# Reordering the opening of a graph layer: transfers, projections and the first matmuls

## The chip, the cores and the metric

The kernel runs on one core of one Trainium2 chip. The metric is the device time in microseconds (us) of one execution. TensorE does the matmuls, VectorE, ScalarE and GpSimd (POOL in the rows) the element-wise work, SyncE (SP) issues the transfers, and 16 DMA engines carry them out.

## The reference

```python
h = item_feat @ W_item.T + b_item            # 10000 x 128
b = x @ W_user.T + b_user                    # 10000 x 128
y = relu(adj @ h + b)                        # adj: 10000 x 10000, float32
m = mean(x + y); v = var(x + y)              # per row
out = (x + y - m) / sqrt(v + 1e-5)
```

Nearly all the work, and nearly all the bytes (400 MB), is `adj @ h`.

## The kernel before, in words

The 10000 users are cut into 20 groups of 500, the 10000 items into 79 chunks of 128 rows (the last has 16). One more chunk holds the user's own projection: `x` stands as its "adj" and `w_user` as its "h". The 80 chunks make 20 tiles of four. One `adj` tile of a group is 128 x 4 x 500 floats, 1.024 MB.

float32 products are made from two float32r halves. ScalarE rounds a tile (`adj_hi`, L301), VectorE subtracts what was rounded (`adj_lo`, L403), and TensorE adds three products for each chunk: hi x hi (L242), lo x hi (L243), and, once `adj_lo` is there, hi x lo (L246). That is `tile_product`. The `h` side is split likewise: ScalarE makes `h_hi` (L342), GpSimd `h_lo` (L367).

`h` is made during group 0. `project_items(t)` (L227) multiplies the four chunks of item tile t by `w_item` into a PSUM bank `h_ps`; VectorE adds the bias into `h_full` (L383), and then the two casts follow. Before, item tile t+2 is projected ahead of the product of tile t, so product 0 has projections 0, 1 and 2 in front of it. The PSUM ring has two banks, `items` two slots, `h_full` three.

What sets the order is each engine's own instruction list, written by hand, with semaphores between the lists. A list is executed in order, so an instruction that waits holds all behind it. SP issues all transfers on one queue. `load_items(t)` waits until the projection that last used its slot is done; `load_adj(g, t)` waits until the `adj_lo` of five tiles earlier is made. One semaphore, `weights_landed`, counts the four small transfers `w_item`, `bias_item`, `w_user` and `bias_user`, and TensorE, ScalarE and VectorE all wait for 64, which is all four.

The results of a group are finished during the next one: relu, adding `x`, transposes by TensorE into `z_ps` with the identity `ident` (L256), statistics, normalisation and the store. Only group 19 does this after the last product. GpSimd makes `ident` at the very start.

## Time and profile before

| | |
|---|---|
| time, median of 3 runs | 1142.09 us (1141.98 to 1143.6) |
| span of the profiled execution, first to last instruction | 1140.9 us |
| the profiled execution's own time | not given apart from its span |
| TensorE busy | 1121.9 us (98%) |
| VectorE, ScalarE, GpSimd busy | 942.8, 805.8, 34.0 us |
| DMA | 415.91 MB, 365 GB/s over the span |
| mean granted TensorE clock | 0.995 |

TensorE's busy time counts from a matmul's start to its modelled end, so a share of 98% says that it hardly ever had nothing queued, not that the array is at its peak. The granted clock is in parts of 2.4 GHz; 0.50 is 1.2 GHz. The "idle before" of a row names what released the engine.

### The profile page before, as it was taken

The page shows a single profiled execution, that of the slowest core. Times are in us where ns is not written, and L with a number is a line of the kernel's source. Part 1 is how long each engine was busy: PE and PEld are TensorE (multiplying, and loading weights), DVE is VectorE, ACT ScalarE, POOL GpSimd, SP SyncE. Part 2 cuts the span into 40 slices and gives each one's busy share as a digit, 9 for nine tenths or more (in the row PEclk, how much of TensorE's full clock was granted, in tenths as well). Part 3 has the DMA queues.
Part 4 walks back from the last instruction along what each step waited for, and adds up shares of the span by engine and source line. Part 5 has one row for each costly group of instructions (what it writes and reads, how often), then busy time and mean ns, then how long its engine had stood idle before and what let it go on. Part 6 is the DMA issues. An engine that isn't in the chain of part 4 may idle for free. (4 is left out here: it accounts for less than half of the span.)

```text
span 1140.9 us, 14807 instructions
## 1 busy us (share of the span) xinstructions
PE 1121.9 (98%) x5038; PEld 931.9 (82%) x5038; DVE 942.8 (83%) x684; ACT 805.8 (71%) x583; POOL 34.0 (3%) x27
## 2 busy tenths in 40 slices
PE   6999999999999999999999999999999999999997
PEld 5888888888888888888888888888888888888885
DVE  4889888888888888888888887888888888888884
ACT  5677767677767777776777777767777777676764
POOL 3440000000000000000000000000000000000000
PEclk8999999999999999999999999999999999999999
DMA  8999999999999999999999999999999999999992
GB/s 297 352 367 402 391 378 368 375 375 378 371 367 382 373 369 379 369 372 374 367 382 365 370 365 392 359 392 362 379 362 387 369 374 368 387 364 366 383 374 78
DMA packets 67471, 415.91 MB, mean 365 GB/s; under 512 B 7872, under 2 KB 11264, under 8 KB 67456
## 3 DMA queue, kind: packets, MB, share of 16 engines
q1 hardware_dynamic: 67456, 415.71, 95.6%
q8 instruction: 9, 0.15, 0.0%
q14 instruction: 6, 0.05, 0.0%
HBM read 410.44 MB, written 5.24 MB: 364 GB/s over the span
## 5 line engine op out<-in xcount | busy, mean ns | idle before, releaser
L403 DVE TENSOR_TENSOR adj_lo<-adj,adj_hi 128x2000 fp32r<-128x2000 f32 (+1 forms) x400 | 873.0, 2191 | 131.1 <-ACT adj_hi L301 130.9
L301 ACT CAST adj_hi<-adj 128x2000 fp32r<-128x2000 f32 (+1 forms) x400 | 730.7, 1827 | 294.3 <-PE acc L246 262.0
L242 PE MATMUL acc<-adj_hi,h_hi 128*128 128x500 f32 x1600 | 630.0, 394 | 0.2 <-POOL h_lo L367 0.2
L243 PE MATMUL acc<-adj_hi,h_lo 128*128 128x500 f32 x1600 | 622.4, 389 | 0.0
L246 PE MATMUL acc<-adj_lo,h_hi 128*128 128x500 f32 x1600 | 429.1, 388 | 0.0
L242 PEld LDWEIGHTS acc<-adj_hi,h_hi 128*128 128x128 f32 x1600 | 301.4, 188 | 63.0 <-POOL h_lo L367 0.5
L246 PEld LDWEIGHTS acc<-adj_lo,h_hi 128*128 128x128 f32 x1600 | 301.1, 188 | 62.1
L243 PEld LDWEIGHTS acc<-adj_hi,h_lo 128*128 128x128 f32 x1600 | 301.9, 189 | 60.6
L418 DVE BATCH_NORM_STATS2 stats<-z_ps 128x6 f32<-128x128 f32 x80 | 17.8, 285 | 32.1 <-PE z_ps L256 32.1
L227 PE MATMUL h_ps<-w_item,items 128*128 128x128 f32 (+1 forms) x158 | 23.3, 296 | 11.1 <-DMA bias_user<-b_user 6.6
L367 POOL TENSOR_TENSOR h_lo<-h_full,h_hi 128x512 fp32r<-128x512 f32 (+1 forms) x20 | 32.8, 1643 | 43.3 <-ACT h_hi L342 43.3
L227 PEld LDWEIGHTS h_ps<-w_item,items 128*128 128x128 f32 (+1 forms) x158 | 22.5, 209 | 12.7 <-DMA bias_user<-b_user 6.6
L383 DVE TENSOR_TENSOR h_full<-h_ps,bias_item 128x512 f32<-128x512 f32 (+1 forms) x20 | 13.6, 678 | 21.6 <-PE h_ps L227 21.6
L320 ACT ACTIVATE normed<-z_ps,shift,rstd 128x128 f32<-128x128 f32 x80 | 29.9, 454 | 0.4 <-DVE shift L436 0.4
L296 ACT CAST adj_hi<-adj 128x500 fp32r<-128x500 f32 x20 | 12.2, 612 | 17.9 <-PE acc L246 17.9
L410 DVE TENSOR_TENSOR z_t<-relu_t,xg 128x500 f32<-128x500 f32 x20 | 13.5, 674 | 7.9 <-ACT relu_t L307 7.9
L307 ACT ACTIVATE relu_t<-acc,bias_user 128x500 f32<-128x500 f32 x20 | 13.4, 671 | 8.8 <-PE acc L246 8.8
L396 DVE TENSOR_TENSOR adj_lo<-adj,adj_hi 128x500 fp32r<-128x500 f32 x20 | 14.3, 715 | 0.0
L342 ACT CAST h_hi<-h_full 128x512 fp32r<-128x512 f32 (+1 forms) x20 | 12.2, 608 | 3.0 <-DVE h_full L383 3.0
L256 PE MATMUL z_ps<-ident,z_t 128*128 128x128 f32 x80 | 12.0, 273 | 1.5 <-DVE z_t L410 1.5
L398 DVE TENSOR_TENSOR adj_lo<-xg,adj_hi 128x500 fp32r<-128x500 f32 x20 | 13.5, 673 | 0.0
L256 PEld LDWEIGHTS z_ps<-ident,z_t 128*128 128x128 f32 x80 | 9.9, 141 | 4.2 <-DVE z_t L410 1.9
(19 smaller groups left out, 37.0 us busy)
## 6 DMA issues: line engine op xcount, KB each, us to landing
adj<-adj_t SPq DMA_DIRECT2D x380, 1000.0 KB, 7.3
adj<-adj_t SPq DMA_DIRECT2D x20, 500.0 KB, 5.5
out<-normed SPq DMA_DIRECT2D x20, 256.0 KB, 7.6
xg<-x_t SPq DMA_DIRECT2D x20, 250.0 KB, 4.4
items<-item_t SPq DMA_DIRECT2D x19, 256.0 KB, 4.7
adj<-adj_tail SPq DMA_DIRECT2D x20, 31.2 KB, 4.8
items<-item_t SPq DMA_DIRECT2D x1, 136.0 KB, 4.5
w_item<-w_item_t SPq DMA_DIRECT2D x1, 64.0 KB, 1.8
```

Source lines behind the costliest of these rows:

```text
L227: mm = nc.tensor.matmul(h_ps[t % 2][0:m, c, :], items[:, t % ITEM_RING, c * P:c * P + m], w_item[:, :], start=True, stop=True)
L242: nc.tensor.matmul(into, h_hi[:, k, :], adj_hi[:, s, c, :], start=(k == 0), stop=False)
L243: nc.tensor.matmul(into, h_lo[:, k, :], adj_hi[:, s, c, :], start=False, stop=False)
L246: mm = nc.tensor.matmul(into, h_hi[:, chunk(t, c), :], adj_lo[:, s, c, :], start=False, stop=(t == LAST and c == PER_TILE - 1))
L256: mm = nc.tensor.transpose(z_ps[:, b, :], z_t[:, b, :], ident[:, :])
L301: nc.scalar.copy(adj_hi[:, s, start:, :], adj[:, a, start:, :]).then_inc(hi_made, 1)
L320: ins = nc.scalar.activation(normed[:, b, :], z_ps[:, b, :], ACT.Identity, bias=shift[:, b:b + 1], scale=rstd[:, b:b + 1])
L367: nc.gpsimd.tensor_tensor(h_lo[:, k:k + n, :], h_full[:, t % H_RING, 0:n, :], h_hi[:, k:k + n, :].bitcast(F32), ALU.subtract).then_inc(h_l ...
L383: ins = nc.vector.tensor_tensor(h_full[:, s, 0:n, :], h_ps[t % 2][:, 0:n, :], bias_item[:, None, :].to_broadcast([P, n, HID]), ALU.add)
L396: nc.vector.tensor_tensor(adj_lo[:, s, AT_TAIL, :], adj[:, a, AT_TAIL, :], adj_hi[:, s, AT_TAIL, :].bitcast(F32), ALU.subtract)
L403: nc.vector.tensor_tensor(adj_lo[:, s, start:, :], adj[:, a, start:, :], adj_hi[:, s, start:, :].bitcast(F32), ALU.subtract).then_inc(lo_m ...
L418: ins = nc.vector.bn_stats(stats[:, b, :], z_ps[:, b, :])
```

## The change

The four small transfers are issued by ScalarE on its own queue, each with a semaphore of its own. SP begins with items 0, 1 and 2, then adj 0, items 3, 4 and 5, adj 1, and from there the items of tile t+4 ahead of adj t. TensorE makes nine transposes of `ident` into `z_ps` as soon as `ident` is ready, waits for `w_item` alone, and projects six item tiles before product 0; later projection t+5 stands ahead of product t. The rings grow: `items` 3, `h_full` 4, `h_ps` 4. VectorE adds the bias of four tiles ahead of the first `adj_lo`, ScalarE casts three `h_full` tiles ahead of the first `adj_hi`. The halves of `w_user` are made with the last tile.

```diff
@@ constants
-ITEM_RING = 2
-H_RING = 3
+ITEM_RING = 3
+H_RING = 4
+H_PS_RING = 4
+LEAD = 6
+WARM = 9
@@ tiles and semaphores
-        h_ps = [psum(f"h_ps{i}", [P, PER_TILE, HID]) for i in range(2)]
+        h_ps = [psum(f"h_ps{i}", [P, PER_TILE, HID]) for i in range(H_PS_RING)]
...
-        weights_landed = sem("weights_landed")
+        w_item_landed = sem("w_item_landed")
+        bias_item_landed = sem("bias_item_landed")
+        w_user_landed = sem("w_user_landed")
+        bias_user_landed = sem("bias_user_landed")
@@ SP
-            sp.dma_start(w_item[:, :], w_item_t).then_inc(weights_landed, 16)
             load_items(0)
-            sp.dma_start(bias_item[:, :], b_item.rearrange("(a n) -> a n", a=1).to_broadcast([P, HID])).then_inc(weights_landed, 16)
             load_items(1)
-            sp.dma_start(w_user[:, :], w_user_t).then_inc(weights_landed, 16)
-            sp.dma_start(bias_user[:, :], b_user.rearrange("(p a) -> p a", a=1)).then_inc(weights_landed, 16)
-            for t in range(TILES):
-                if t >= ITEM_RING:
-                    load_items(t)
+            load_items(2)
+            load_adj(0, 0)
+            load_items(3)
+            load_items(4)
+            load_items(5)
+            load_adj(0, 1)
+            for t in range(2, TILES):
+                if t + LEAD - 2 < TILES:
+                    load_items(t + LEAD - 2)
                 if t == LOAD_X_AT:
                     load_x(0)
                 load_adj(0, t)
@@ TensorE
-                if t >= 2:
-                    pe.wait_ge(h_full_made, t - 1)
+                if t >= H_PS_RING:
+                    pe.wait_ge(h_full_made, t - H_PS_RING + 1)
...
-            pe.wait_ge(weights_landed, 64)
-            project_items(0)
-            project_items(1)
+            def warm_up():
+
+                for b in range(WARM):
+                    nc.tensor.transpose(z_ps[:, b % BLOCKS, :], ident[:, :], ident[:, :])
+
+            pe.wait_ge(ident_ready, 1)
+            warm_up()
+            pe.wait_ge(w_item_landed, 16)
+            for t in range(LEAD):
+                project_items(t)
             for t in range(TILES):
-                if t + 2 < TILES:
-                    project_items(t + 2)
+                if 1 <= t and t + LEAD - 1 < TILES:
+                    project_items(t + LEAD - 1)
                 if t == LAST:
                     pe.wait_ge(w_lo_made, 1)
                 pe.wait_ge(h_lo_made, t + 1)
                 tile_product(0, t, 0)
-            pe.wait_ge(ident_ready, 1)
@@ ScalarE
-            act.wait_ge(weights_landed, 64)
-            nc.scalar.copy(h_hi[:, CHUNKS - 1, :], w_user[:, :]).then_inc(w_hi_made, 1)
+            def split_h(t):
+
+                n = item_chunks(t)
+                act.wait_ge(h_full_made, t + 1)
+                nc.scalar.copy(h_hi[:, t * PER_TILE:t * PER_TILE + n, :],
+                               h_full[:, t % H_RING, 0:n, :]).then_inc(h_hi_made, 1)
+
+            act.dma_start(w_item[:, :], w_item_t).then_inc(w_item_landed, 16)
+            act.dma_start(bias_item[:, :], b_item.rearrange("(a n) -> a n", a=1).to_broadcast([P, HID])).then_inc(bias_item_landed, 16)
+            act.dma_start(w_user[:, :], w_user_t).then_inc(w_user_landed, 16)
+            act.dma_start(bias_user[:, :], b_user.rearrange("(p a) -> p a", a=1)).then_inc(bias_user_landed, 16)
+            for t in range(LEAD - 3):
+                split_h(t)
             act.wait_ge(pads_ready, 1)
             for t in range(TILES):
+                if t == LAST:
+                    act.wait_ge(w_user_landed, 16)
+                    nc.scalar.copy(h_hi[:, CHUNKS - 1, :], w_user[:, :]).then_inc(w_hi_made, 1)
+                    act.wait_ge(bias_user_landed, 16)
                 split_hi(0, t)
...
+                if t + LEAD - 3 < TILES:
+                    split_h(t + LEAD - 3)
@@ GpSimd: the h_lo of w_user moves behind the loop over tiles
@@ VectorE
-            dve.wait_ge(weights_landed, 64)
-            add_item_bias(0)
-            add_item_bias(1)
+            dve.wait_ge(bias_item_landed, 16)
+            for t in range(LEAD - 2):
+                add_item_bias(t)
             for t in range(TILES):
                 split_lo(0, t)
-                if t + 2 < TILES:
-                    add_item_bias(t + 2)
+                if t + LEAD - 2 < TILES:
+                    add_item_bias(t + LEAD - 2)
```

The first rows of SP's list before; the names are destination and source of each transfer, and "waits" the semaphore:

```order
L198 DMA w_item<-w_item_t 128x128
L169 DMA items<-item_t 128x512
L200 DMA bias_item<-b_item 128x128
L169 DMA items<-item_t 128x512
L202 DMA w_user<-w_user_t 128x128
L203 DMA bias_user<-b_user 128x1
L178 DMA adj<-adj_t 128x2000 x2
L169 DMA items<-item_t 128x512 [waits h_product]
L178 DMA adj<-adj_t 128x2000
```

And SP's list now, to the same depth:

```order
L175 DMA items<-item_t 128x512 x3
L184 DMA adj<-adj_t 128x2000
L175 DMA items<-item_t 128x512 [waits h_product] x3
L184 DMA adj<-adj_t 128x2000
L175 DMA items<-item_t 128x512 [waits h_product]
L184 DMA adj<-adj_t 128x2000
```

The small transfers are gone from it, one adj tile instead of two stands ahead of the first items that wait for a projection (`h_product`), and three items stand between adj 0 and adj 1.

TensorE's list before, from its start to the lo part of product 0:

```order
L227 MATMUL h_ps<-w_item,items 128x128 [waits item_landed0,weights_landed]
L227 MATMUL h_ps<-w_item,items 128x128 x3
L227 MATMUL h_ps<-w_item,items 128x128 [waits item_landed1]
...
L227 MATMUL h_ps<-w_item,items 128x128 [waits h_full_made,item_landed0]
...
L242 MATMUL acc<-adj_hi,h_hi 128x500 [waits hi_made,h_lo_made]
...
L246 MATMUL acc<-adj_lo,h_hi 128x500 [waits lo_made]
```

The same stretch now:

```order
L278 MATMUL z_ps<-ident 128x128 [waits ident_ready]
L278 MATMUL z_ps<-ident 128x128 x8
L235 MATMUL h_ps<-w_item,items 128x128 [waits item_landed0,w_item_landed]
...
L235 MATMUL h_ps<-w_item,items 128x128 [waits item_landed1]
...
L235 MATMUL h_ps<-w_item,items 128x128 [waits item_landed2]
...
L235 MATMUL h_ps<-w_item,items 128x128 [waits item_landed0]
...
L235 MATMUL h_ps<-w_item,items 128x128 [waits h_full_made,item_landed1]
...
L235 MATMUL h_ps<-w_item,items 128x128 [waits h_full_made,item_landed2]
...
L250 MATMUL acc<-adj_hi,h_hi 128x500 [waits hi_made,h_lo_made]
...
L254 MATMUL acc<-adj_lo,h_hi 128x500 [waits lo_made]
```

Three projections moved ahead of product 0, the nine transposes ahead of everything, and the first projection now waits for `w_item` where it waited for all four small transfers.

## Rows read from the trace of the kernel before

**Rows 1.** The page, part 1: busy time, share of the span, instructions.
```profile
PE 1121.9 (98%) x5038; PEld 931.9 (82%) x5038; DVE 942.8 (83%) x684; ACT 805.8 (71%) x583; POOL 34.0 (3%) x27
```

**Rows 2.** Waits of the whole run: engine, line, releaser: us in total, times, longest.
```profile
ACT adj_hi L301 <- PE acc L246: 262.0, 328, 1.2
...
PE h_ps L227 <- DMA bias_user<-b_user: 6.6, 1, 6.6
...
PE h_ps L227 <- DMA items<-item_t: 4.5, 1, 4.5
```

**Rows 3.** Stretches: length, busy (instructions) per engine, granted clock, DMA share, GB/s.
```profile
0.00:10.00 10.00, 3.37 (x16) 3.25 (x16) 1.24 (x3) 1.58 (x2) 1.16 (x7) 1.00 0.69 201
10.00:20.00 10.00, 5.30 (x17) 4.38 (x17) 6.28 (x4) 7.11 (x6) 4.63 (x3) 0.66 1.00 399
13.00:14.00 1.00, 0.00 (x0) 0.00 (x0) 0.58 (x1) 1.00 (x3) 0.01 (x1) 0.50 0.98 408
17.00:19.00 2.00, 2.00 (x5) 1.66 (x6) 2.00 (x2) 2.00 (x2) 1.04 (x1) 0.50 0.96 323
21.82:82.35 60.53, 60.53 (x333) 52.42 (x332) 49.58 (x36) 39.26 (x37) 25.70 (x17) 1.00 0.96 351
```

**Rows 4.** Timeline of the opening: start, length, engine, line, operation, idle before.
```profile
1.19 0.29 POOL L357 TENSOR_SCALAR_AFFINE_SELECT ident<-ident 128x128 f32<-128x128 f32 x1 [0.24 <-POOL ident L355]
...
3.55 0.91 SPq L178 DMA_DIRECT2D adj<-adj_t  x2
...
11.53 1.86 ACT L301 CAST adj_hi<-adj 128x2000 fp32r<-128x2000 f32 x1 [4.62 <-DMA adj<-adj_t]
...
13.42 2.24 DVE L403 TENSOR_TENSOR adj_lo<-adj,adj_hi 128x2000 fp32r<-128x2000 f32 x1 [2.62 <-ACT adj_hi L301]
...
13.99 4.05 POOL L367 TENSOR_TENSOR h_lo<-h_full,h_hi 128x512 fp32r<-128x512 f32 x2 [6.54 <-ACT h_hi L342]
```

**Rows 5.** Timeline of TensorE alone, 6 to 22 us.
```profile
6.63 3.44 PE L227 MATMUL h_ps<-w_item,items 128*128 128x128 f32 x16 [6.63 <-DMA bias_user<-b_user]
14.55 2.07 PE L227 MATMUL h_ps<-w_item,items 128*128 128x128 f32 x8 [4.47 <-DMA items<-item_t]
16.85 0.78 PE L242 MATMUL acc<-adj_hi,h_hi 128*128 128x500 f32 x1 [0.23 <-POOL h_lo L367]
...
20.11 1.06 PE L246 MATMUL acc<-adj_lo,h_hi 128*128 128x500 f32 x4
```

**Rows 6.** Timeline of TensorE alone, later: tile periods and four transposes.
```profile
21.82 0.48 PE L242 MATMUL acc<-adj_hi,h_hi 128*128 128x500 f32 x1
...
23.72 1.06 PE L246 MATMUL acc<-adj_lo,h_hi 128*128 128x500 f32 x4
...
25.43 0.47 PE L242 MATMUL acc<-adj_hi,h_hi 128*128 128x500 f32 x1
...
82.35 0.39 PE L242 MATMUL acc<-adj_hi,h_hi 128*128 128x500 f32 x1
...
85.07 0.39 PE L242 MATMUL acc<-adj_hi,h_hi 128*128 128x500 f32 x1
...
106.87 0.60 PE L256 MATMUL z_ps<-ident,z_t 128*128 128x128 f32 x4
107.22 0.47 PE L242 MATMUL acc<-adj_hi,h_hi 128*128 128x500 f32 x1
```

**Rows 7.** DMA issues at 1.2, 0.8, 3.6 and 8.7 us: KB, us to landing.
```profile
items<-item_t SPq DMA_DIRECT2D x1, 256.0 KB, 2.8
...
w_item<-w_item_t SPq DMA_DIRECT2D x1, 64.0 KB, 1.8
...
adj<-adj_t SPq DMA_DIRECT2D x1, 1000.0 KB, 7.9
...
items<-item_t SPq DMA_DIRECT2D x1, 256.0 KB, 5.8
```

**Rows 8.** The page, part 5: busy, mean ns, idle before.
```profile
L383 DVE TENSOR_TENSOR h_full<-h_ps,bias_item 128x512 f32<-128x512 f32 (+1 forms) x20 | 13.6, 678 | 21.6 <-PE h_ps L227 21.6
```

More of the change, by code:

```diff
@@ L222, in project_items @@
                 pe.wait_ge(item_landed[t % ITEM_RING], 16 * (t // ITEM_RING + 1))
-                if t >= 2:
-                    pe.wait_ge(h_full_made, t - 1)
+                if t >= H_PS_RING:
+                    pe.wait_ge(h_full_made, t - H_PS_RING + 1)
                 for c in range(item_chunks(t)):
                     m = min(P, N_ITEM - (t * PER_TILE + c) * P)
-                    mm = nc.tensor.matmul(h_ps[t % 2][0:m, c, :], items[:, t % ITEM_RING, c * P:c * P + m],
+                    mm = nc.tensor.matmul(h_ps[t % H_PS_RING][0:m, c, :], items[:, t % ITEM_RING, c * P:c * P + m],
                                           w_item[:, :], start=True, stop=True)
@@ L332, in group @@
                         normalise(g - 1)
-            act.wait_ge(weights_landed, 64)
-            nc.scalar.copy(h_hi[:, CHUNKS - 1, :], w_user[:, :]).then_inc(w_hi_made, 1)
+            def split_h(t):
[9 more added lines that the diff above has]
+                split_h(t)
             act.wait_ge(pads_ready, 1)
             for t in range(TILES):
+                if t == LAST:
+                    act.wait_ge(w_user_landed, 16)
+                    nc.scalar.copy(h_hi[:, CHUNKS - 1, :], w_user[:, :]).then_inc(w_hi_made, 1)
+                    act.wait_ge(bias_user_landed, 16)
                 split_hi(0, t)
-                act.wait_ge(h_full_made, t + 1)
-                n = item_chunks(t)
-                nc.scalar.copy(h_hi[:, t * PER_TILE:t * PER_TILE + n, :],
-                               h_full[:, t % H_RING, 0:n, :]).then_inc(h_hi_made, 1)
+                if t + LEAD - 3 < TILES:
+                    split_h(t + LEAD - 3)
             group(1, 1)
@@ L358, in _ @@
                                     base=0, pattern=[[-1, P]], channel_multiplier=1).then_inc(ident_ready, 1)
-            pool.wait_ge(w_hi_made, 1)
-            nc.gpsimd.tensor_tensor(h_lo[:, CHUNKS - 1, :], w_user[:, :], h_hi[:, CHUNKS - 1, :].bitcast(F32),
-                                    ALU.subtract).then_inc(w_lo_made, 1)
             for t in range(TILES):
@@ L368, in _ @@
                                         h_hi[:, k:k + n, :].bitcast(F32), ALU.subtract).then_inc(h_lo_made, 1)
+            pool.wait_ge(w_hi_made, 1)
+            nc.gpsimd.tensor_tensor(h_lo[:, CHUNKS - 1, :], w_user[:, :], h_hi[:, CHUNKS - 1, :].bitcast(F32),
+                                    ALU.subtract).then_inc(w_lo_made, 1)
         @block.vector
@@ L382, in add_item_bias @@
                 dve.wait_ge(h_product, t + 1)
-                ins = nc.vector.tensor_tensor(h_full[:, s, 0:n, :], h_ps[t % 2][:, 0:n, :],
+                ins = nc.vector.tensor_tensor(h_full[:, s, 0:n, :], h_ps[t % H_PS_RING][:, 0:n, :],
                                               bias_item[:, None, :].to_broadcast([P, n, HID]), ALU.add)
                 if t == LAST:
-                    ins = nc.vector.tensor_tensor(h_full[0:TAIL, s, n, :], h_ps[t % 2][0:TAIL, n, :],
+                    ins = nc.vector.tensor_tensor(h_full[0:TAIL, s, n, :], h_ps[t % H_PS_RING][0:TAIL, n, :],
                                                   bias_item[0:TAIL, :], ALU.add)
```

## The prediction

> **What bounds the kernel now.** I read the busy shares first: TensorE works 1121.9 us of a span of 1140.9 us, and its weight loads, VectorE and ScalarE less [rows 1]. A high share alone does not make a bound, so the waits come next [rows 2]: TensorE waits for a transfer twice, 6.6 + 4.5 = 11.1 us, both before product 0, while ScalarE waits for TensorE 328 times (262.0 us). From the first product on, TensorE never waits for anything, so the time is the start of product 0, plus the work queued behind it, plus a tail after the last product. The change touches only the first of these and, a little, the second. The stretches show the same: 0 to 10 and 10 to 20 us hold 3.4 and 5.3 us of TensorE's work, 21.82 to 82.35 is full [rows 3].
>
> The opening in order of time [rows 4, 5]: SP issues four small transfers, items 0 and 1 and two adj tiles, the tiles in 0.91 us (0.46 each), adj 0 at 3.55. TensorE waits for the last of the four (bias_user) until 6.63, projects items 0 and 1 in 3.44 us, then idles until items 2 lands at 14.54 behind adj 0 and adj 1, projects it in 2.07 us and starts product 0 at 16.85. POOL's first h_lo pair ran from 13.99 to 18.04, and it was released by ScalarE's h_hi, itself behind the cast of adj 0.
>
> The clock: the granted share is 0.50 in 13 to 14 us, 3 us after the last matmul (10.07), though 0.66 over 10 to 20 [rows 3], and the matmuls are back at the full pace near 20 [rows 5]. A warm projection takes 0.89 us more of TensorE: a product with one has a period of 3.61 us (21.82 to 25.43), one without 2.72 us (82.35 to 85.07) [rows 6]. At half clock a projection took 2.07 us [rows 5]. Projections 0 and 1 took 3.44 us, so they too began at the half-speed pace, though the column shows 1.00 there; by that pace I reckon the clock as down at the start. The Trainium skill, "TensorE: Matmul & The Clock Gate", section "Seeing it yourself", says the clock records should be cross-checked and not trusted one by one; the pace of rows 5 bears it out.
>
> **The change part by part.**
>
> *Reference point.* Product 0 began at 16.85, and its eight hi matmuls lasted to 20.11, 3.26 us, against 1.90 us warm (21.82 to 23.72) [rows 5, 6]: 1.36 us lost to the clock. Three projections were done. The changed kernel has six done when product 0 starts, so three fewer come later: 3 x 0.89 = 2.67 us. Before is thus worth a warm product 0 at 16.85 + 1.36 + 2.67 = 20.88 us. Whatever time T the changed kernel starts product 0 at, warm, the gain is 20.88 - T.
>
> *Warm-up.* ident is ready at 1.19 + 0.29 = 1.48 us [rows 4]. Four transposes took 0.35 us at full clock (106.87 to 107.22) [rows 6], so nine are 0.79 us, or 1.58 us at half: over by 3.1 us, before any item is there. They cost nothing on the path. What they can give is an earlier rise of the clock.
>
> *Weights on ScalarE's queue.* Items 0 is issued at 0.75 instead of 1.19 and took 2.8 us to land [rows 7]: 3.55 us, and TensorE no longer waits for bias_user at 6.6. The wait is now for w_item (1.8 us to land, [rows 7]) and items 0. I take 3.7. All four small ones had landed by 6.63, so bias_item, the second, is there for VectorE after projection 0. ScalarE's four issues, at 0.46 us each, end near 2.6 us, long before h_full 0 exists. Projection 0 at half clock: 3.7 to 5.8; projection 1 to 7.9 at worst, projection 2 to 8.9 (items 1 and 2, issued at 1.2 and 1.7, land near 4.7 and 5.8: 2.8 us of [rows 7] and 0.66 us for each 256 KB ahead, at the 399 GB/s of [rows 3]). The w_user cast and its h_lo move from the head of ScalarE and POOL to the last tile: one cast and one subtraction of a quarter of a bias add's size (0.68 us, [rows 8]) on engines that are not the bound; nothing.
>
> *The wait that takes the place of the old ones.* The items buffer has three slots, so items 3 is issued only after projection 0, when adj 0 is long queued. Items 2 of before, issued with two adj tiles queued ahead, took 5.8 us to land against the 2.8 of items 0 [rows 7]. So items 3, 4 and 5 land behind adj 0. Adj 0 landed at 3.55 + 7.9 = 11.45. It is now issued at 2.16, with 256 KB more ahead of it. If issue time decides: 11.45 - 1.39 + 0.66 = 10.7. If the bytes do: 11.45 + 0.66 = 12.1. I take 11.2, nearer the first since two queues start in parallel. Items 3, 4, 5: 11.9, 12.5, 13.2. TensorE idles from about 8.9 to 11.9.
> The 16 engines were 0.69 busy in 0 to 10 us and full in 10 to 20 [rows 3]. The Trainium skill, "DMA: Bandwidth & Descriptors", section "Issuing engines are not separate DMA queues", says that transfers of different issuers share the same 16 engines, and a second issuer saves only the issue time; by it the weights still cost the items their packets, which speaks for the upper of the two ends, 12.1, and 0.9 us less gain.
>
> *Projections 3 to 5.* Warm: 11.9 + 3 x 0.89 = 14.6. All at half clock: 11.9 + 3 x 2.07 = 18.1. Before, the clock was down 2.9 us after the last matmul and back some 5.3 us after work resumed at 14.55 [rows 3, 5]. The new gap is about as long as that fall took, so I take a fall. With the return 5.3 us after 11.9, at 17.2, two and a half projections run cold and T is 17.6. Before, that resumption was broken twice by waits and here three projections follow each other, so I expect it sooner and take T = **16.6**, between the warm 14.6 and the cold 18.1, nearer the latter.
> Weighed beside it stands the Trainium skill, "TensorE: Matmul & The Clock Gate", section "HAM oscillation — how this bites in real kernels": bursts of matmuls between waits for DMAs start cold each time. It speaks against the warm-up, since the gap after projection 2 would undo it; the fall at 13 in rows 3 agrees.
>
> *Is product 0 ready then?* h_lo 0: projection 0 done 5.8, bias add 0.7 [rows 8], the cast no more than that, POOL 2.0 us (4.05 for two, [rows 4]): 9.2. ScalarE casts adj 0 from 11.2 to 13.1; VectorE's lo follows the bias add of projection 3 (at 14.0 + 0.7) and takes 2.24 [rows 4]: 17.0, needed at 16.6 + 1.9 = 18.5. Yes.
>
> *Is the supply in time after that?* A tile with its items is 1.286 MB: 3.22 us at 399 GB/s [rows 3], 3.66 us at the 351 of the long stretch [rows 3]. Adj 1 lands near 15.8 (13.2 + 1.024 MB), cast by 17.7, needed at 16.6 + 3.6 = 20.2. The slack of 2.5 us then changes by -0.06 to +0.4 us a tile. No stall.
>
> *Sum.* 20.88 - 16.6 = 4.3 us. The end is unchanged: the same tail after the last product. Durations come from a profiled span of 1140.9 us, 1.2 us under the median of 1142.09; no separate time of that execution is shown, so I subtract from both alike: span 1136.6, time **1137.8 us**.
>
> **Rivals.**
> 1. *The clock stays up through the gap* (or the gap is shorter). T = 14.6, gain 6.3, time 1135.8. For it: more work before the gap than before had; against: the fall after 2.9 us of idling [rows 3]. With adj 0 at 10.7 it is 1135.3.
> 2. *The supply eats it.* The DMA rate was 323 GB/s in 17 to 19 us [rows 3]. A tile with items then takes 3.98 us, 0.38 over TensorE's period; over 14 such tiles 5.3 us, less the slack of 2.5: 2.8 us of stalls, seen as TensorE waiting for adj_hi. Gain 1.5, time 1140.6. Against: 399 GB/s over 10 to 20 us as a whole.
> 3. *Slower: the small transfers come late on ScalarE's queue.* If w_item is released no earlier than the last of the small ones was (6.6) and the projections start there at half clock, items 3 is issued at 8.8, and lands 5.8 us later, as items 2 of before did: 14.6. Three projections at 2.07 and a cold product 0 give 14.6 + 6.2 + 1.4 = 22.2 against 20.88: 1.3 us slower, 1143.4; with the 7.9 us that adj 0 took, 1145.5. It decides from a product 0 later than 20.88. Against: w_item alone took 1.8 us.
> 4. *The change does nothing for the clock and T is 18.1 or more with a cold product 0*: 18.1 + 1.4 = 19.5, gain 1.35, 1140.7. It shares its price with rival 2.
>
> **How the numbers follow.** About 0.2% (2.3 us, what a measurement here can tell from no change) is 1139.8 on the fast side. Forecast, clock down and back: 45%, own range 1136.8 to 1139.4 (T 15.6 to 18.1). Rival 1: 27%. Rivals 2 and 4: 22%. Rival 3: 6%. Faster: 45 + 27 + 4 of the third group = 76%; same 18%; slower 6%. The range takes the forecast, rival 1 to 1135.0 and the nearer half of rivals 2 and 4, up to 1140.6.
>
> **What the new profile would show.** Nine transposes from 1.5 us; the first projection near 3.7 and no wait for bias_user; then one wait of TensorE for DMA items, about 3 us, ending near 11.9; a second fall of the clock during it; product 0 at 16.6, its hi part 1.9 us long, not 3.3; the last product 4.3 us earlier. The prediction is wrong if TensorE waits for adj_hi or items after product 0, if product 0 starts before 14.5 or after 18.5, or if the last matmul moves by another amount than product 0 plus 2.67 us.

## The result and the profile after

| | before | after |
|---|---|---|
| median, range, runs | 1143.01 us (1141.98 to 1152.16), 13 | 1137.34 us (1135.98 to 1139.4), 13 |
| runs of 1149 us or more | 3 | 0 |
| span of the profiled run; its own time | 1140.9 us | 1135.4 us; 1137.26 us |
| TensorE, GpSimd busy | 1121.9, 34.0 us | 1122.6, 56.2 us |

The changed kernel is faster: ratio 0.9924, 95% interval 0.9902 to 0.9947. The ratio of the two medians is 0.9950 (5.67 us less) and that of the two means 0.9933; the three long runs of before pull the others below the medians' ratio. So two things are to be explained, 5.45 us in the pair of profiles and the long runs that only before has. Among the experiments below, one run of experiment 10 took 1595.17 us at a mean granted clock of 0.654 and is left out.

Where the 5.45 us lie is told by one instruction in every group, the four transposes by TensorE. Group 0's began at 106.87 us in before [rows 6]. After's, and its last ones of the run (before's last began at 1134.09), on TensorE's timeline:

```profile
101.40 0.60 PE L264 MATMUL z_ps<-ident,z_t 128*128 128x128 f32 x4
...
1128.64 0.66 PE L264 MATMUL z_ps<-ident,z_t 128*128 128x128 f32 x4 [1.48 <-DVE z_t L437]
```

The lead is 5.47 us after group 0 and 5.45 us at the end: all of it was made in group 0, and nothing later moved. TensorE's timeline of the opening, after (start, length, engine, line, operation, idle before and its releaser), to be held against rows 5:

```profile
1.53 2.18 PE L278 MATMUL z_ps<-ident 128*128 128x128 f32 x9 [1.53 <-POOL ident L384]
4.04 4.60 PE L235 MATMUL h_ps<-w_item,items 128*128 128x128 f32 x24 [0.32 <-DMA w_item<-w_item_t]
10.74 2.94 PE L235 MATMUL h_ps<-w_item,items 128*128 128x128 f32 x24 [2.10 <-DMA items<-item_t]
13.44 0.48 PE L250 MATMUL acc<-adj_hi,h_hi 128*128 128x500 f32 x1
...
15.34 1.06 PE L254 MATMUL acc<-adj_lo,h_hi 128*128 128x500 f32 x4
17.30 1.16 PE L235 MATMUL h_ps<-w_item,items 128*128 128x128 f32 x8 [0.90 <-DMA items<-item_t]
18.64 0.47 PE L250 MATMUL acc<-adj_hi,h_hi 128*128 128x500 f32 x1 [0.18 <-ACT adj_hi L315]
...
20.82 1.17 PE L254 MATMUL acc<-adj_lo,h_hi 128*128 128x500 f32 x4
21.83 1.05 PE L235 MATMUL h_ps<-w_item,items 128*128 128x128 f32 x8
22.64 0.47 PE L250 MATMUL acc<-adj_hi,h_hi 128*128 128x500 f32 x1
```

Product 0 starts at 13.44 where before's started at 16.85 [rows 5], its hi part lasts 1.90 us (to 15.34), full pace. Product 2 starts at 22.64. Without a wait it would have started two periods of 3.61 us [rows 6] after 13.44, at 20.66; so 1.98 us were lost again. By the prediction's yardstick the gain is 20.88 - 13.44 - 1.98 = 5.46 us, and 5.45 is what the transposes show. What released ScalarE's casts, same stretch:

```profile
7.48 1.30 ACT L353 CAST h_hi<-h_full 128x512 fp32r<-128x512 f32 x2 [3.56 <-DVE h_full L410]
...
10.13 1.86 ACT L315 CAST adj_hi<-adj 128x2000 fp32r<-128x2000 f32 x1
...
16.64 1.86 ACT L315 CAST adj_hi<-adj 128x2000 fp32r<-128x2000 f32 x1 [3.36 <-DMA adj<-adj_t]
...
19.75 1.87 ACT L315 CAST adj_hi<-adj 128x2000 fp32r<-128x2000 f32 x1 [0.74 <-DMA adj<-adj_t]
```

Two things stand there. The h casts now run at 7.48, ahead of the cast of adj 0, while in before h_lo 0 was only released at 13.99, behind it [rows 4]. And adj 1 lands at 16.6, which is what delays products 1 and 2. The stretches of the same run (length, busy time and instructions per engine, granted clock, DMA share, GB/s), against rows 3:

```profile
4.00:6.00 2.00, 1.96 (x9) 1.88 (x9) 0.00 (x0) 0.00 (x0) 0.00 (x0) 1.00 0.68 150
6.00:8.00 2.00, 1.91 (x13) 1.72 (x13) 1.25 (x2) 0.52 (x1) 0.00 (x0) 1.00 1.06 423
...
9.00:10.00 1.00, 0.00 (x0) 0.00 (x0) 0.37 (x1) 0.60 (x1) 1.00 (x2) 1.00 1.05 378
10.00:11.00 1.00, 0.26 (x2) 0.27 (x3) 0.00 (x0) 0.89 (x2) 1.00 (x2) 1.00 1.07 306
...
13.00:15.00 2.00, 2.00 (x14) 1.77 (x13) 2.00 (x2) 0.28 (x1) 1.65 (x1) 1.00 0.93 282
```

The clock column stays at 1.00 through TensorE's idle time from 8.64 to 10.74, where before shows 0.50 three microseconds after its last matmul [rows 3]. The column alone would not do (it shows 1.00 beside the first nine transposes too, which take 2.18 us, the half pace), but the matmuls behind the gap bear it out: three projections in 2.94 us, the full pace. And the rate is 150 GB/s in 4 to 6 us and 282 in 13 to 15, not the 399 that the prediction used. The waits of the whole run (engine, line, releaser: us in total, times, longest):

```profile
ACT adj_hi L315 <- PE acc L254: 266.4, 334, 1.3
...
ACT adj_hi L315 <- DMA adj<-adj_t: 18.3, 20, 3.4
```

ScalarE still waits for TensorE 334 times: past group 0 the bound is what it was [rows 2].

### The profile page after: what moved, and what is told of

Read it like the earlier page. It is cut to its first block and busy times, and to the rows that moved or that the text cites. A ratio compares the mean times of both kernels' runs of the same rounds, so it can differ in the third digit from the quotient of the medians.

```text
span 1135.4 us, 14822 instructions
## 1 busy us (share of the span) xinstructions
PE 1122.6 (99%) x5047; PEld 931.5 (82%) x5047; DVE 945.4 (83%) x684; ACT 806.9 (71%) x583; POOL 56.2 (5%) x27
## 5 line engine op out<-in xcount | busy, mean ns | idle before, releaser
L391 POOL TENSOR_TENSOR h_lo<-h_full,h_hi 128x512 fp32r<-128x512 f32 (+1 forms) x20 | 54.2, 2714 | 15.5 <-ACT h_hi L353 15.5
```

Source lines behind the costliest of these rows:

```text
L391: nc.gpsimd.tensor_tensor(h_lo[:, k:k + n, :], h_full[:, t % H_RING, 0:n, :], h_hi[:, k:k + n, :].bitcast(F32), ALU.subtract).then_inc(h_l ...
```

## Experiments

The theory after the first comparison: two chains stood in front of before's product 0 and ended nearly together, items 2 behind two adj tiles, and h_lo 0 behind ScalarE's cast of adj 0; the change removes both. After product 0 the bytes decide. Rivals: the warm-up does it (through the clock), the moved weights do it, or the earlier items alone do it. "T" is the start of product 0; "shift" is how much earlier than in before's profile the last transposes start (after: 5.45 us).

| variant | median us (range), runs | ratio, 95% interval | T us | shift us |
|---|---|---|---|---|
| the change | 1137.34 (1135.98 to 1139.4), 13 | 0.9924, 0.9902 to 0.9947 | 13.44 | 5.45 |
| 1 no warm-up | 1137.34 (1136.01 to 1138.39), 12 | 0.9936, 0.9912 to 0.9959 | 15.78 | 4.46 |
| 2 before with warm-up | 1142.98 (1141.46 to 1152.51), 12 | 1.0005, 0.9976 to 1.0035 | 16.94 | -6.87 |
| 3 before, weights by ScalarE | 1143.76 (1142.84 to 1153.53), 12 | 0.9993, 0.9964 to 1.0022 | 16.65 | -1.31 |
| 4 lead 3, no early cast | 1143.71 (1143.07 to 1145.47), 12 | 0.9979, 0.9952 to 1.0006 | 17.11 | -1.47 |
| 5 lead 3, one early cast | 1143.42 (1142.78 to 1144.14), 12 | 0.9984, 0.9958 to 1.001 | 12.26 | -0.17 |
| 6 lead 6, no early cast | 1141.46 (1140.72 to 1142.93), 12 | 0.9964, 0.9937 to 0.999 | 17.34 | 0.25 |
| 7 lead 8 | 1139.06 (1138.12 to 1139.74), 12 | 0.9935, 0.9907 to 0.9963 | 17.43 | 3.16 |
| 8 before, lead grows later | 1143.67 (1143.0 to 1144.58), 12 | 0.9967, 0.9939 to 0.9994 | 16.61 | -1.89 |
| 9 items 3 to 5 not loaded | 1134.75 (1134.45 to 1135.83), 6 | 0.9898, 0.9859 to 0.9937 | 13.59 | 6.88 |
| 10 as 5, w_user early | 1148.54 (1147.8 to 1150.4), 11 | 1.0025, 0.9997 to 1.0052 | 13.16 | -6.27 |
| 11 lead 4, then 6 | 1137.17 (1136.29 to 1137.93), 9 | 0.9915, 0.9886 to 0.9945 | 12.55 | 4.77 |
| 12 lead 5 | 1137.09 (1135.63 to 1138.11), 8 | 0.9922, 0.989 to 0.9954 | 14.30 | 5.33 |

Before's own median beside them was 1143.04, 1143.0 and 1143.05 us (35, 35 and 22 runs), with 10, 12 and 8 of those runs at 1149 or more. Its remaining runs in them have a median of 1142.3 to 1142.7; above those variants 3, 4, 5 and 8 lie 1.1 to 1.4 us, though their ratios, which count the long runs too, lie below 1.

**1. Without the warm-up.**

```
-WARM = 9
+WARM = 0
```

> The changed kernel without the nine transposes. Theory A (the warm-up brought the clock up by 6.6 us and kept it there, which is half of what the prediction missed): TensorE starts at 4.0 us cold, projections 0 to 2 end near 9.5 instead of 8.6, the clock is still down or falls again in the wait for items 3, projections 3 to 5 and the first part of product 0 run at half pace, product 0 starts at 15 to 17 us instead of 13.4, and the end is 1.0 to 3.0 us later than with them, a gain over before of 2.5 to 4.5 us. Rival theory S (after product 0 the supply of adj and items sets the pace, so an earlier product 0 is partly given back): product 0 also starts late, but the waits of about 2 us behind product 0 shrink by as much, and the end moves by less than 1 us, gain still 4.5 to 6.

The median is the same to 0.01 us. Its trace shows why little is lost: TensorE's timeline without the warm-up.

```profile
4.15 5.35 PE L235 MATMUL h_ps<-w_item,items 128*128 128x128 f32 x24 [4.15 <-DMA w_item<-w_item_t]
11.15 2.05 PE L235 MATMUL h_ps<-w_item,items 128*128 128x128 f32 x16 [1.65 <-DMA items<-item_t]
14.86 1.16 PE L235 MATMUL h_ps<-w_item,items 128*128 128x128 f32 x8 [1.66 <-DMA items<-item_t]
15.78 0.47 PE L250 MATMUL acc<-adj_hi,h_hi 128*128 128x500 f32 x1
...
23.64 0.47 PE L250 MATMUL acc<-adj_hi,h_hi 128*128 128x500 f32 x1
```

The first three projections take 5.35 us against 4.60, the wait for items 5 brings product 0 to 15.78 (2.34 us later than with the warm-up), but product 2, at 23.64, is only 1.00 us later: the transfers decide by then, and they let the earlier start wait. In the pair of profiles the warm-up is worth that 1.0 us, in the medians nothing. So T came where theory A had it, and the end where theory S had it.

**2. Before, with the nine transposes.**

```
+            pe.wait_ge(ident_ready, 1)
+            for b in range(9):
+                nc.tensor.transpose(z_ps[:, b % BLOCKS, :], ident[:, :], ident[:, :])
             pe.wait_ge(weights_landed, 64)
```

> The kernel before with nine transposes of the identity at its start and nothing else. TensorE then idles from 3.7 to 6.6 us, and again from about 9.5 to 14.5. Theory A: the clock that a warm-up brings does not outlive these idle stretches, product 0 still starts between 16.3 and 16.9 and partly cold; gain 0 to 0.7 us. Rival (the warm-up alone carries the gain through the clock): product 0 warm from its first matmul, gain 1.4 to 2.5 us.

No change, 1.0005, as theory A had it. Product 0 starts at 16.94, no earlier. Its profiled run happened to be one of the long ones (1149.56 us; the others took 1151.63 to 1152.51), and so shows what the profile of before does not: of the 6.87 us that its last transposes come later, 0.41 are there at product 1 (22.23 against 21.82) and 6.4 are lost at the end of group 0. GpSimd, VectorE and TensorE at the end of group 0 in that run, one fence each:

```profile
75.10 1.91 POOL L369 TENSOR_TENSOR h_lo<-h_full,h_hi 128x512 fp32r<-128x512 f32 x1 [1.68 <-ACT h_hi L344]
81.00 8.27 POOL L369 TENSOR_TENSOR h_lo<-h_full,h_hi 128x512 fp32r<-128x512 f32 x2 [3.99 <-ACT h_hi L344]
```

```profile
83.99 7.37 DVE L405 TENSOR_TENSOR adj_lo<-adj,adj_hi 128x1000 fp32r<-128x1000 f32 x3
```

```profile
81.87 1.07 PE L246 MATMUL acc<-adj_lo,h_hi 128*128 128x500 f32 x4
86.36 0.79 PE L242 MATMUL acc<-adj_hi,h_hi 128*128 128x500 f32 x1 [3.42 <-POOL h_lo L369]
86.94 0.62 PE L243 MATMUL acc<-adj_hi,h_lo 128*128 128x500 f32 x1
```

The last two h_lo, 1.29 and 1.91 us in before's profile, take 8.27 us beside VectorE's subtractions, which follow each other without a pause there (80.67 to 91.37); TensorE waits 3.42 us, and its matmuls then run at half pace (0.62 us each, not 0.39; granted clock 0.77 in 80 to 90 us and 0.89 in 90 to 100). In the change GpSimd has its last h_lo of items done at 71.2 us, some 8 us before it is used. Call this loss E. That before's own long runs lose their time in the same place is inferred from this one trace; none of them has a trace of its own.

What may have tipped this run stands on ScalarE: it had waited 3.52 us for the adj tile that it casts at 78.54 (1.09 us for the same tile in before's profile, cast at 76.81). So h_lo 18 began at 81.00, after VectorE had begun its run, where before's began at 79.28, in a pause, and was done at 80.57. One trace does not show that a late transfer is the rule.

The Trainium skill, "GPSIMD Engine Reference", section "1. Specifications", says that GpSimd's SBUF interfaces are shared with VectorE and that an instruction of VectorE with two SBUF inputs contends for them; adj_lo is such an instruction, and the 8.27 us agree.

**3. Before, with the four weights on ScalarE's queue** and the w_user halves last, as in the change.

```
-            pe.wait_ge(weights_landed, 64)
+            pe.wait_ge(w_item_landed, 16)
...
+            act.dma_start(w_item[:, :], w_item_t).then_inc(w_item_landed, 16)
```

> The kernel before with the four small transfers on ScalarE's queue with semaphores of their own, and w_user's halves made with the last tile; order of items, adj and projections as before, no warm-up. Projection 0 starts at 4.0 instead of 6.6 and adj 0 is issued at 1.7 instead of 3.6. Theory Q (the transfer queue, not the wait for the weights, sets product 0): items 2 stands behind adj 0 and adj 1, which land about 1.5 us earlier, so product 0 starts at 15 to 15.5 cold; gain 1.0 to 2.0 us. Rival (all of the 2.6 us of the lost wait arrive): gain 2.6 us or more.

```profile
4.02 2.07 PE L226 MATMUL h_ps<-w_item,items 128*128 128x128 f32 x8 [4.02 <-DMA w_item<-w_item_t]
6.92 2.08 PE L226 MATMUL h_ps<-w_item,items 128*128 128x128 f32 x8 [0.82 <-DMA items<-item_t]
13.17 2.08 PE L226 MATMUL h_ps<-w_item,items 128*128 128x128 f32 x8 [4.18 <-DMA items<-item_t]
16.65 0.79 PE L241 MATMUL acc<-adj_hi,h_hi 128*128 128x500 f32 x1 [1.40 <-POOL h_lo L369]
```

Projection 0 starts at 4.02 instead of 6.63 and product 0 at 16.65 instead of 16.85: the earlier start buys nothing, where theory Q expected 15 to 15.5. Items 2 still lands behind the adj tiles, and with that moved to 13.17 the other chain shows, a wait of 1.40 us for h_lo 0. That chain has grown by something the edit did not mean: ScalarE loads its function table (ACT_TABLE_LOAD, 1.28 us) ahead of its first cast. Before's first cast is that of w_user, and the load was over at 2.02; here it is that of adj 0, and the load runs from 10.03, when adj 0 has landed, to 11.31. Without it h_lo 0 would have come up to 1.28 us earlier, about where theory Q had it; no run tests that. The half pace also lasts longer than in before (the four lo matmuls at 20.15 take 1.87 us, 1.06 in [rows 5]), and product 1 starts at 23.12, 1.30 us later than before's.

**4. The change, with only three projections and no h cast ahead of adj 0's.**

```
-LEAD = 6
+LEAD = 3
+BIAS_LEAD = 1
+CAST_LEAD = 0
```

> The changed kernel with three projections ahead of product 0 instead of six, as before had: SP issues items 0 to 2, adj 0, adj 1, then items t+1 ahead of adj t; VectorE adds one bias and ScalarE makes no cast ahead. Warm-up and weights as changed. Theory S (supply bound): product 0 can start near 12 us when adj 0 is cast, adj 1 lands 1.9 us earlier (14.7 instead of 16.6), the waits behind product 0 vanish or become short, and the end is within 1 us of the change with six, gain 4.7 to 6.5 us. Rival L (the lead of six is worth its 3 projections of 0.89 us): 2.0 to 2.7 us later than with six, gain 3 to 3.7.

```profile
4.03 5.06 PE L236 MATMUL h_ps<-w_item,items 128*128 128x128 f32 x24 [0.31 <-DMA w_item<-w_item_t]
17.11 0.78 PE L251 MATMUL acc<-adj_hi,h_hi 128*128 128x500 f32 x1 [8.02 <-POOL h_lo L392]
```

ScalarE there:

```profile
10.51 1.28 ACT L316 ACT_TABLE_LOAD   x1 [10.51 <-DMA adj<-adj_t]
```

All three projections are done at 9.09 and yet product 0 starts at 17.11: TensorE waits 8.02 us for h_lo 0, whose cast stands on ScalarE behind that of adj 0 (11.80 to 13.66) and whose subtraction then takes 2.80 us. Both theories missed: neither had h_lo 0 in it. The table load is on the chain again, 1.28 of the 8.02 us. Experiment 4 takes the wall of items 2 away and 3 moves it 1.4 us ahead, and in both the other wall stands within 0.3 us of before's 16.85; but without the table load it would have stood up to 1.28 us earlier in either. So the wall of h_lo 0 is shown, and that one edit alone gains nothing is in part the work of the load.

**5. Lead 3, with one h cast ahead of adj 0's.**

```
-CAST_LEAD = 0
+CAST_LEAD = 1
-BIAS_LEAD = 1
+BIAS_LEAD = 2
```

> The variant with three projections, but VectorE adds two biases and ScalarE makes h_hi 0 ahead of its cast of adj 0. Theory W (two walls stood in front of product 0 before: items 2 behind two adj tiles, and h_lo 0 behind ScalarE's wait for adj 0; taking one away shows only the other): the 8.0 us wait of TensorE for POOL's h_lo disappears, product 0 starts at 12.0 to 13.0 instead of 17.1, and the end is 2.5 to 5.5 us earlier than without the early cast: 1138.2 to 1141. Rival L (the lead of six itself is what pays): still above 1142.5.

With both walls gone, TensorE alone, opening and end of group 0:

```profile
12.26 0.76 PE L251 MATMUL acc<-adj_hi,h_hi 128*128 128x500 f32 x1 [3.46 <-ACT adj_hi L316]
...
17.23 0.48 PE L251 MATMUL acc<-adj_hi,h_hi 128*128 128x500 f32 x1
...
83.51 0.78 PE L251 MATMUL acc<-adj_hi,h_hi 128*128 128x500 f32 x1 [2.86 <-POOL h_lo L395]
84.09 0.62 PE L252 MATMUL acc<-adj_hi,h_lo 128*128 128x500 f32 x1
```

Product 0 starts at 12.26, product 1 at 17.23, 4.59 us before that of before (21.82, [rows 6]) with the same number of projections still to come. That is as expected; the end was not (1138.2 to 1141). The number is the rival's, but not for the rival's reason: at the end of the run nothing of the 4.59 us is left, loss E takes it at 83.51, 2.86 us of waiting and 3.4 us at half pace behind it. The range of its runs is 1.4 us wide, so by the times it came in all of them. Lead 3 opens nearly as well as the change does (4.6 of 5.5 us) and pays at the other end of the group. Its T is also 4.85 us earlier than that of experiment 4; 1.28 of them are the table load, which the early cast puts at 2.63 again.

**6. Lead 6, no early h cast.**

```
+BIAS_LEAD = 4
+CAST_LEAD = 0
```

> The changed kernel with ScalarE's three casts of h_full behind its cast of adj 0 again, one h_hi behind each adj_hi; all else as changed, six projections. Theory W: h_lo 0 comes 2.6 us or more after the cast of adj 0 at 12.0, so product 0 starts at 15 to 16.5 instead of 13.4, but about 2 us of that lie inside the waits for supply that follow it anyway; the end is 0.5 to 2 us later than the change: 1138 to 1139.4. Rival L: no difference to the change (within 0.4 us).

Product 0 at 17.34, after 1.68 us of waiting for h_lo, and product 1 at 22.95 after 1.74 more; 4.1 us slower than the change, twice the most that was expected. This is the step that the prediction left out, the h casts taken ahead of the adj casts, measured by itself: with six projections ahead it is worth 4.1 us. In the profiles the two differ by 5.20 us: 3.96 are there at product 2 (26.60 against 22.64), and 1.2 more are lost towards the end of group 0. T holds the 1.28 us of table load here too, but product 1 does not: it waits for h_lo 1, which follows the landing (17.63) and the cast of adj 1. No run reached 1149.

**7. Lead 8.**

```
-LEAD = 6
+LEAD = 8
```

> The changed kernel with eight projections ahead of product 0 (items 3 to 7 between adj 0 and adj 1); biases and casts ahead as changed. Theory S (supply): adj 1 lands 1.3 us later, product 0 starts near 15.3, TensorE's waits after it stay about as long, since a projection gives 0.89 us of work for 0.66 us of transfer; the end is within 0.6 us of the change. Rival L: 1.8 us earlier than the change (two more projections).

SP's queue, opening:

```profile
2.13 0.43 SPq L186 DMA_DIRECT2D adj<-adj_t  x1
6.17 7.34 SPq L177 DMA_DIRECT2D items<-item_t  x5
13.55 0.43 SPq L186 DMA_DIRECT2D adj<-adj_t  x1
```

Five items in a row now stand ahead of adj 1, and with three slots the last of them is only issued when projections have freed one. Adj 1 is issued at 13.55, against 9.04 in the change, and ScalarE waits 6.91 us for it. 1.7 us slower than the change, where neither theory had it. By these rows the cost is the order on SP's queue, adj 1 behind items that wait for a slot.

**8. Before's opening, the lead growing to six from product 1 on.** (Rings as in the change.)

```
-                if t + 2 < TILES:
-                    project_items(t + 2)
+                for k in ahead(t, 1, (2, 4, 6, 8), 5):
+                    project_items(k)
```

`ahead` gives the projections that bring the lead to 2, 4, 6, 8 at products 0 to 3, then 5 ahead of each.

> The kernel before, its opening as it was (three projections, adj 0 and 1 ahead of items 2, casts behind adj_hi), but from product 1 on the projections, biases and casts run further ahead, until they are as far ahead as in the changed kernel. Theory P (part of what the median and the fast runs of before lose is at the other end of group 0: in 10 of 35 runs before took 1149 to 1153 us, because POOL's h_lo 18 is starved by VectorE's subtractions and TensorE waits for it): none of the 12 or so runs is above 1146, while the typical run stays at 1142 to 1143.5. Rival (those runs come from the opening, or from outside the kernel): runs above 1149 go on, in about three of ten.

Product 0 starts cold at 16.61 and the shift is -1.89 us, so its opening is no better than before's. But none of its 12 runs reached 1149, where before had 12 of 35. If 12 of 35 were its odds too, 12 runs without one would come 0.6% of the time (23/35 to the 12th). The last h_lo starts at 76.13 and lasts 2.71 us. So loss E goes without a better opening, as theory P had it, by what experiment 8 changed behind product 0: the lead, with larger rings. That it is the lead alone is not shown: experiment 4, with the same rings, lead 3 and the halves of w_user last, had no run of 1149 among 12 either, and no wait for h_lo at the end of group 0 in its profile.

**9. The change, items 3 to 5 not loaded and not waited for.** Projections 3 to 5 use what stands in the slots; 0.79 MB less is moved, and that part of h is not the reference's.

```
-            load_items(3)
-            load_items(4)
-            load_items(5)
```

> The changed kernel without the loads of items 3, 4 and 5 (0.79 MB); projections 3 to 5 read what lies in the slots, so that part of h is not the reference's. All instructions of the engines stay. Theory S (TensorE waits for bytes in the opening): the 2.1 us wait for items 3 goes, product 0 starts near 12.1 (when adj 0 is cast) instead of 13.4, adj 1 lands near 14.0 to 14.7 instead of 16.6, and the 1.7 us of waits between product 0 and the lo part of product 1 go; the end is 2.5 to 3.8 us earlier than the change, 1133.5 to 1134.8. Rival (the waits come from the order of the engines' lists, not from bytes): product 0 moves by 1.3 us at most and the waits behind it stay, 1136 or more.

```profile
6.51 6.48 PE L233 MATMUL h_ps<-w_item,items 128*128 128x128 f32 x40 [0.40 <-DMA items<-item_t]
13.59 0.46 PE L248 MATMUL acc<-adj_hi,h_hi 128*128 128x500 f32 x1 [0.59 <-ACT adj_hi L313]
...
21.20 0.47 PE L248 MATMUL acc<-adj_hi,h_hi 128*128 128x500 f32 x1
```

Product 0 is not earlier (13.59; 12.1 was expected), but product 2 starts at 21.20 instead of 22.64: two periods after 13.59 would be 20.81, so 0.39 us are lost there and not 1.98. The median falls by 2.6 us, as expected, more than the 1.4 us of the profiled pair. What was lost after product 0 is supply: take these transfers out and most of it goes. Whether it is their bytes or their place in the list is not separated here, since without them SP issues adj 1 right behind adj 0, not at 9.04; experiments 7 and 11 bear on that.

**10. Experiment 5, with the w_user halves early, nearly as in before** (GpSimd makes its half behind h_lo 0).

```
+            act.wait_ge(w_user_landed, 16)
+            nc.scalar.copy(h_hi[:, CHUNKS - 1, :], w_user[:, :]).then_inc(w_hi_made, 1)
...
-                if t == LAST:
-                    act.wait_ge(w_user_landed, 16)
-                    nc.scalar.copy(h_hi[:, CHUNKS - 1, :], w_user[:, :]).then_inc(w_hi_made, 1)
```

> e5 (three projections, one early cast) with the two halves of w_user made at the start again, as in the kernel before, instead of with the last tile. Theory P (POOL, slowed beside VectorE's subtractions, makes TensorE wait at the end of group 0, and the clock then falls): POOL's h_lo of w_user at 81.0 to 83.5 held TensorE for 2.9 us in e5 and the half pace behind it cost about 1.5 more; with it gone TensorE waits 0 to 0.8 us for h_lo 19, the clock stays up, and of the 4.6 us by which product 1 of e5 was early 3.5 to 4.6 arrive at the end: 1138.4 to 1139.6. Rival: the early opening is lost elsewhere and the end stays above 1142.

A miss of 9 us: I took w_user's subtraction, the last in the queue, for the cause of the end's loss, and without it there the loss was greater. GpSimd, VectorE and TensorE there:

```profile
77.22 11.13 POOL L391 TENSOR_TENSOR h_lo<-h_full,h_hi 128x384 fp32r<-128x384 f32 x1 [0.75 <-ACT h_hi L354]
```

```profile
79.86 7.64 DVE L431 TENSOR_TENSOR adj_lo<-adj,adj_hi 128x1000 fp32r<-128x1000 f32 x4
```

```profile
88.45 0.76 PE L251 MATMUL acc<-adj_hi,h_hi 128*128 128x500 f32 x1 [6.93 <-issue]
89.00 0.62 PE L252 MATMUL acc<-adj_hi,h_lo 128*128 128x500 f32 x1
```

h_lo 19, three quarters of a full one, takes 11.13 us, and ends only when VectorE's run of subtractions has ended (87.5). The TensorE row names no releaser, but it starts 0.1 us after that h_lo ends at 88.35. In experiment 5 it began just as it does here, 0.7 us into VectorE's last full subtraction (76.36 after 75.66, here 77.22 after 76.53), and was done in 4.69 us, with VectorE's row going on to 87.7. And in the change, where it starts 8 us earlier in the group, it took 2.73 us:

```profile
68.44 2.73 POOL L391 TENSOR_TENSOR h_lo<-h_full,h_hi 128x384 fp32r<-128x384 f32 x1 [0.26 <-ACT h_hi L353]
```

There too VectorE's subtractions follow each other without a pause (67.75 to 75.69), but the second of them took 3.06 us, where those of experiment 10 kept 2.22: in the change GpSimd got in between two of them, in experiment 10 it did not. So the place of loss E is shown, and that GpSimd made little way there beside VectorE's subtractions; that taking VectorE's subtractions away would end it was not tried. What decides whether GpSimd gets in between, and with it the size of the loss, is open, and so is whether the moved w_user made it larger.

**11 and 12. Lead 4 growing to 6, and lead 5.**

```
-LEAD = 6
+LEAD = 5
```

> A mix: four projections ahead of product 0, two more ahead of each of products 1 and 2, then one, so that the lead is six from product 2 on; two early casts, three early biases. Theories S and P together: product 0 starts near 12.3 as in e5, the end of group 0 is safe as in the change, and bytes still bound the opening, so that it is within 0.8 us of the change and faster if anything: 1136.3 to 1137.5. Rival L (each projection ahead pays 0.89 us): 1.8 us slower than the change, 1139.1.

> The changed kernel with five projections ahead of product 0 and throughout, three early biases, two early casts. Theory S: product 0 starts near 12.5, adj 1 lands 0.6 us earlier than with six; the end is within 0.6 us of the change, 1136.7 to 1137.9, and no run shows the loss at the end of group 0. Rival L: 0.9 us slower, 1138.2.

Both are what the change is, within 0.3 us (1137.17 and 1137.09), as expected. Experiment 11 starts product 0 earliest of the three, at 12.55, and has product 2 at 21.95, with as many projections done as the change has at 22.64; but its product 3 starts at 26.41 (26.23 in the change) and product 4 at 30.42 (29.83), behind late items and a late adj tile. Its adj 1 is issued at 6.50 and has landed by 13.59, 3 us before the change's, and the end is the same: what comes early here is paid for by what comes behind it, which speaks for the bytes. None of these beats the change by more than the spread of its runs.

Experiment 12 shows one thing more, in projections 3 and 4:

```profile
11.07 3.48 PE L236 MATMUL h_ps<-w_item,items 128*128 128x128 f32 x16 [2.06 <-DMA items<-item_t]
```

The gap is 2.06 us, as in the change (2.10), and here the clock did fall: the column shows 0.50 from 11 to 14 us, and two projections take 3.48 us where the change has three in 2.94. It is the same in experiment 6 (2.05 us of waiting, then 4.45 us for three). So that the clock stayed up through the change's gap belongs to the run that was profiled and cannot be counted on. T is 14.30 for it, where 12.5 was expected. But product 2 starts at 21.79 with one projection less done than in the change; with 0.89 us for it that is 22.68, against 22.64. The fall costs T and nothing after it, since the transfers decide by then.

## Why the prediction was right and wrong

**Bound and place: right.** What group 0 gains arrives at the end: the shift is 5.47 us after group 0 and 5.45 at the end.

**"Before is worth a warm product 0 at 20.88": right.** 20.88 - 13.44 - 1.98 gives 5.46 against 5.45.

**Warm-up: right that it costs nothing.** It took 2.18 us, not 0.79 to 1.58, still over at 3.71. What it gives was left open; experiment 1 puts it at nothing in the median.

**Weights on ScalarE's queue: right in what matters.** The first projection was to start at 3.7 and did at 4.04. The small ones landed later than the forecast had it (w_item 3.3 us after its issue, against 1.8 in rows 7; bias_item 5.5), and VectorE waited 5.31 us for bias_item, but product 0 was not waiting for that chain. Rival 3, the only slower one, asked for a projection 0 at 6.6 and did not come.

**"Then one wait for DMA items, ending near 11.9": right in kind.** It was 2.10 us, ending at 10.74. Adj 0 landed at 10.03, 7.9 us after its issue at 2.13 (forecast 11.2, between 10.7 and 12.1), so even the lower bound was too high: in this pair the landing went with the issue, not with the bytes ahead (in experiments 3, 4 and 6 it took 8.3 to 8.4 us).

**"The new gap is about as long as that fall took, so I take a fall": this step failed.** The gap was 2.10 us, the column stayed at 1.00, projections 3 to 5 took 2.94 us and T was 13.44, not 16.6. That is rival 1's mechanism, with the items 1.2 us earlier still. The largest error, 3.2 us: 1.2 from the items and 2.0 from the clock. The step reasoned from one fall and took the length of the gap as what decides; the runs show gaps of equal length going both ways (2.10 us here, 2.05 and 2.06 with a fall in experiments 6 and 12). The term for the fall was also too dear: 2.07 us is one cold projection by itself, while two in a row, mostly cold, took 3.44 [rows 5] and 3.48 in experiment 12. And a fall would not have made the end later by as much as T: in experiment 12 nothing of it is left at product 2.

**"No stall" after product 0: this step failed too**, in the other direction. Adj 1 was cast at 16.64, not after landing at 15.8, and that with product 0 3.2 us ahead of the forecast: 1.98 us were lost. Rival 2 had named the wait, but priced it by a rate of 323 GB/s over 14 tiles; it lasted two tiles, at 282 GB/s in 13 to 15 us. The two errors, 3.2 us one way and 2.0 the other, leave 5.45 us against the 4.3 forecast: that they are so near is luck. By the prediction's own signs it was wrong: T lay before 14.5, TensorE waited for items and adj_hi after product 0, and the end moved by 5.45 us, not by product 0's 3.41 plus 2.67.

**The h casts ahead of adj 0's were in the working only as a check** ("Is product 0 ready then?"), with no price. Experiments 4, 5 and 6 show them to be one of two walls: 4.1 us with six projections ahead. They also kept ScalarE's table load of 1.28 us ahead of adj 0's landing, which the prediction had not counted. The yardstick hid this, since it asks only when product 0 starts and not what else held it back. Had only the transfers and projections been reordered, the time would have been experiment 6's 1141.46, 3.7 us above the forecast.

**The end of the group was costed at nothing ("on engines that are not the bound; nothing").** The move of w_user cost nothing in the change, but loss E was missed altogether. Three of before's first 13 runs took some 9 us more than the rest, by the trace of experiment 2 in that place, and none of the change's did: this is why the measured ratio lies below what the profiled pair gives (0.9952). This term, put at nothing, is the larger part of what the forecast gain lacked. The profiled run of before had been spared it; the only trace of it in the rows was the h_lo of 4.05 us for two at 13.99 [rows 4] against 1.3 for one later in the group, read as a duration and not as a warning.

**Numbers.** The median of 1137.34 lies 0.5 us under the forecast 1137.8 and within 1135.0 to 1140.6. The gain in medians is 5.67 us, and by the ratio 8.7 us (0.0076 of 1143; 6.1 to 11.2 by the interval), where 4.3 was forecast: the time was near, by luck, and the change of the time was too small.

**Left open.** What decides whether the clock falls in a gap of 2 us; what experiments 3 and 4 would give with the table load kept early; why the rate is only 150 GB/s in 4 to 6 us and 282 in 13 to 15; whether w_user and bias_user, loaded later, would let the items land sooner (not tried); and what decides in which runs of before loss E comes (a late adj tile is the one candidate that a trace shows).

## What to carry to other kernels

When a kernel's first heavy operation has several inputs, write down when each of them is ready before pricing an edit: of two chains that end within 0.3 us of each other, taking one away can show no more than those 0.3 us, and both together gave 4.6 (product 1 of experiment 5). Look too at what an edit makes the first instruction of an engine: a one-time load of 1.28 us moved with it here. Ask the same at the far end of the phase: a slow helper engine that keeps pace by a small margin needs a lead there, and if single runs of a kernel lie some microseconds above the rest, the profiled run may not show why. An earlier start is worth only as much as the transfers behind it can follow.

## What the runs showed of the hardware

- GpSimd's 128x512 subtraction took 1.3 us alone and 2.6 to 3.1 us beside VectorE's subtractions. Where those followed each other without a pause, one of 128x384 took 2.73 us (the change), 4.69 (experiment 5) and 11.13 (experiment 10), and one of each size in a row 8.27 (experiment 2).
- Waits of 2.10 us (the change) and 1.65 us (experiment 1) between matmuls left the granted clock at 1.00; after waits of 2.05 and 2.06 us (experiments 6 and 12) it was 0.50 and the matmuls at half pace; waits of 2.86, 3.42, 3.46 and 6.93 us were each followed by matmuls of 0.62 us, the pace of 1.2 GHz.
- Nine transposes or none at the start: the median was 1137.34 us both ways.
- ScalarE's first ACT_TABLE_LOAD took 1.28 us. It ran at 0.74 us in before and 2.64 in the change, while the first cast still waited; in experiments 3, 4 and 6, whose first cast is that of adj 0, it ran only at 10.03, 10.51 and 10.61, when adj 0 had landed.
- The four small transfers took longer on ScalarE's queue, with items issued on SP's at the same time: 3.3, 5.5, 5.9 and 8.1 us instead of 1.8, 3.3, 3.1 and 3.5. Which of the two made them slower was not tested.
